# A small clear on GpSimd behind each gather of the last layer

## What is computed

```python
s = node_feats @ msg_w[:, :D].T
d = node_feats @ msg_w[:, D:].T
messages = gelu(s[:, None, :] + d[None, :, :] + msg_b)       # for each pair (i, j)
aggregated = einsum('ijd,ij->id', messages, adj)              # adj is mostly zero
new_feats = concatenate([node_feats, aggregated]) @ upd_w.T + upd_b
h = gelu(new_feats) + node_feats
x = layernorm(x + (layernorm(h) * ln_w + ln_b))
```

## Time and profile before

| | |
|---|---|
| median of three timed runs | 707.23 us |
| span of the profiled execution | 785.9 us |
| GpSimd busy in the profiled span | 333.8 us |
| VectorE busy in the profiled span | 480.0 us |

### The profile page before, as it was taken

How to read it: one execution, slowest core, us unless ns; L and a number is a source line. 1 busy time by engine, 2 the same in 40 slices (tenths; PEclk the granted TensorE clock), 3 DMA queues, 4 the chain that set the end, 5 groups by cost and what they waited for, 6 DMA issues and landing times.

```text
span 785.9 us, 6700 instructions
## 1 busy us (share of the span) xinstructions
PE 445.2 (57%) x1987; PEld 269.0 (34%) x1987; DVE 480.0 (61%) x1457; ACT 301.0 (38%) x363; POOL 333.8 (42%) x492
## 2 busy tenths in 40 slices
PE   4221118999999999999843855304504404405231
PEld 4121113444455655444632734203303303303120
DVE  2419608988946569523454559539849749748564
ACT  3565364458823316995611302203213213213131
POOL 7204502555522126400055356726636736736700
PEclk9555555999999999999865886656757757757655
DMA  8999992999712124990022211211112112111200
GB/s 317 367 424 420 398 324 110 365 398 387 298 71 72 56 72 156 425 374 1 28 73 56 73 44 43 54 30 51 47 37 50 52 32 51 50 33 50 54 8 13
DMA packets 32697, 117.20 MB, mean 149 GB/s; under 512 B 8518, under 2 KB 19636, under 8 KB 23892
## 3 DMA queue, kind: packets, MB, share of 16 engines
q1 hardware_dynamic: 19970, 78.21, 25.3%
q0 software_dynamic: 9952, 38.49, 15.5%
q10 hardware_dynamic: 2734, 0.01, 0.2%
HBM read 111.15 MB, written 5.55 MB: 148 GB/s over the span
## 4 chain that ended last, share of the span: by engine, by line
PE 40%; DVE 25%; DMA 11%; issue 10%; another core or an unknown queue 8%; ACT 3%; SPq 1%; ACTq 0%; DVEq 0%
PE ps L122 38%; DMA ring<-in_adjT_dram 11%; DVE agg L1858 4%; DVE G L1855 3%; DVE G L1843 2%; DVE A L1747 1%; DVE st L1761 1%; DVE M L1725 1%; SPq L842 1%; DVE Mh L1724 1%; DVE t L1779 1%; DVE t L1782 1%; DVE t L1781 1%; DVE yo L1788 1%
## 5 line engine op out<-in xcount | busy, mean ns | idle before, releaser
L939 POOL DMA_INDIRECT G<-near,IX x147 | 140.3, 954 | 44.8 <-issue 44.8
L122 PE MATMUL ps<-ident,agg 128*128 128x128 f32 (+1 forms) x44 | 14.3, 420 | 192.6 <-DVE agg L1858 160.2
L122 PE MATMUL ps<-ring,hwu 128*128 128x512 f32 (+3 forms) x264 | 114.3, 586 | 1.0 <-ACT hwu L1032 1.0
L122 PE MATMUL ps<-ring,xT_s 128*128 128x512 f32 (+1 forms) x264 | 108.0, 553 | 0.0
L1522 DVE FIND_INDEX8 I<-V,rows 128x8 uint32<-128x452 f32 (+1 forms) x132 | 82.1, 627 | 0.0
L939 POOL DMA_INDIRECT Go<-near,IO x44 | 43.6, 990 | 89.7 <-DVE IO L1741 59.5
L1532 DVE MAX8 V<-rows 128x8 f32<-128x452 f32 (+1 forms) x132 | 79.9, 618 | 0.8
L122 PEld LDWEIGHTS ps<-ident,agg 128*128 128x128 f32 (+1 forms) x44 | 9.4, 260 | 198.2 <-DVE agg L1858 162.6
L122 PEld LDWEIGHTS ps<-ring,hwu 128*128 128x128 f32 (+1 forms) x264 | 51.0, 203 | 63.9 <-issue 62.7
L1019 ACT ACTIVATE binT<-ring 128x2708 bf16<-128x2708 f32 (+1 forms) x22 | 53.9, 2459 | 45.2 <-DMA ring<-in_adjT_dram 45.2
L1039 ACT ACTIVATE binT<-ring 128x2708 bf16<-128x2708 f32 (+1 forms) x22 | 53.9, 2456 | 29.5 <-PE ps L122 29.5
(11 more groups left out here) (258 smaller groups left out, 843.9 us busy)
## 6 DMA issues: line engine op xcount, KB each, us to landing
ring<-in_adjT_dram SPq DMA_DIRECT2D x46, 1354.0 KB, 15.5
rows<-in_adj_dram POOLq DMA_DIRECT2D x17, 1354.0 KB, 9.5
rows<-in_adj_dram SPq DMA_DIRECT2D x4, 1354.0 KB, 23.7
G<-near,IX POOLq DMA_INDIRECT x147
xT_s<-in_xT_dram SPq DMA_DIRECT2D x1, 1354.0 KB, 6.3
near<-hwu SPq DMA_DIRECT2D x1, 1344.0 KB
out_dram<-yo SPq DMA_DIRECT2D x21, 64.0 KB
near2f<-hwu SPq DMA_DIRECT2D x5, 256.0 KB
```

Source lines behind the costliest of these rows:

```text
L122: return pe.matmul(dst, lhsT, rhs, start=start, stop=stop, skip_group_check=True)
L939: pool.indirect_dma_start(out=dst, out_offset=None, in_=table, in_offset=bass.IndirectOffsetOnAxis(ap=index, axis=0), engine_sem=o_g).then ...
```

## The change

A buffer `spare` of 128 partitions x 2 x 128 float32 is added. Behind each of the 191 gathers of layer 3 GpSimd clears one half of it (64 KB in all partitions together), the halves in turn. Each clear counts up `o_look`, and from the third on it waits first for the clear two before it (which used the same half). Nothing reads `spare`. The 22 gathers of layer 2 are as before.

```diff
+        spare = sb("spare", [P, 2, P])
...
+            pauses = itertools.count()
+
+            def pause():
+
+                k = next(pauses)
+                if k >= 2:
+                    pool.wait_ge(o_look, 9 * NB + k - 1)
+                pool.memset(spare[:, k % 2, :], 0.0).then_inc(o_look, 1)
+
             pool.wait_ge(s_n3, 16 * len(GROUPS2))
             for g in range(NG3):
...
                 for k in range(CAP):
                     gather(Go[:, g % 2, k, :], near3[:, :], IO[:, g, k:k + 1], s_go[g % 2])
+                    pause()
...
                     for k in range(TOP):
                         gather(G3[0:rn(n), n % QUEUE3, k, :], near3[:, :], IX[0:rn(n), n, k:k + 1], s_g[n % QUEUE3])
+                        pause()
```

More of the change, by code:

```diff
@@ L1 @@
+import itertools
 from contextlib import ExitStack
```

## The result

Six runs of the changed kernel have a median of 727.82 us (724.76 to 729.75), beside 707.44 us (706.32 to 710.78) for six runs of the kernel before. The ratio on record is 1.0262, 95% interval 1.023 to 1.0294, which is 18.5 us of 707.44; the two medians are 20.4 us apart. The forecast was slower, by 38 us, to 745.

A forecast was written before the change was run, and what follows sets the result against it. GpSimd's gathers (line 695.8 us) and VectorE's pairs (691) were taken to bound the kernel nearly together, GpSimd later. 191 clears x 0.20 = 38.2 us on 707.2 gave 745; likeliest range 730 to 768, 8 in 10 from 706 to 785.

The forecast's parts named there:

- The line drawn for GpSimd: GpSimd's layer 3 gathers from 434.8, 191 at 1.25 us, then 1.8 landing and 20.4 to the end: 695.8 us.
- The 11.4 us: Timed median above GpSimd's line of 695.8 us, taken as time lying around the span.
- the 78.7 us: First profile's span of 785.9 us over the timed median 707.2, taken as stalls where gathers are issued, nearly absent when timed.
- the late signals: Unnamed waits where gathers are issued, 95 us in the first profile, put down to the recording and the density of gathers.
- rival (c): Faster: late signals are real in timed runs too and the clear thins them out; 655 us, chance 0.12.
- I take 0.20 us on top of 1.25: Layer 3 gathers on GpSimd: each clear adds 0.20 us to the 1.25 between gather starts, pitch 1.45.
- rival (a): Clear hidden in the 0.30 us between gathers, or VectorE's 21.3 us pairs hold the pace: 707, up to 3 more; chance 0.18.
- (b): Clear costs twice, needing another 0.30 us gap beside an indirect DMA: 0.50 x 191 = 95.5, 803 us; chance 0.12.
- Hold-ups: Clears and VectorE's instructions delaying each other: at most 3.6 us a pair, covered by VectorE's 4.8 us to spare.
- 191 x: All 191 layer 3 clears counted at full cost on GpSimd's line: 191 x 0.20 = 38.2 us.
- the new wait: VectorE waits for a gather's landing ahead of L1843, some 4.8 us in each pair of blocks.
- The length of a pair: Two blocks of layer 3, 18 gathers: 18 x 1.45 = 26.1 us, against VectorE's 21.3.

The follow-up runs named there:

- six-gather kernel: Kernel before with the seventh gather left out for each block from block 6 on, without clears: 697.39 us, ratio 0.9854 to the kernel before.
- the second profile: The kernel before, nothing edited, profiled a second time: span 708.7 us, execution 710.41 us.

## Why the prediction was right and wrong

**Who bounds the kernel: right.** GpSimd's gathers set the pace, VectorE nearly does. The six-gather kernel shows it: 10 us go with the gathers, and VectorE's 21.25 us takes over. The line drawn for GpSimd was too short, though. It ended at 695.8; the second profile has 439.2 for the first gather (not 434.8), 172 pitches of 1.28 with the hold-ups (not 191 of 1.25) and 49.5 us behind them, 708.7 in all. The 11.4 us that I took to lie around the span are 1.7 (708.7 and 710.41).

**Where the 78.7 us lie: the use was right, the reason wrong.** I took the late signals as absent from the timed kernel, and they are. I put them down to the recording of unbroken gathers, and expected them again, if weaker, in the changed profile. Two more profiles of kernels with the gathers of before (708.7 and 705.8 us, the latter with the range tests exchanged) have none. They were of one execution. What delayed the signals there stays open; no other profile has them (whether the unprofiled execution of 2313.47 us had, can't be said), and rival (c), which lived on them, had nothing to stand on. The Trainium skill, Runtime: NRT & Kernel Launch, section The launch sequence, puts a profile's total 6.2 us above the reported time in every kernel. I had set this case's 78.7 us against it, and that was no fair test, since they were of one execution. The spans here, from first to last instruction, lie 1.8 and 1.7 us below the times (727.0 and 728.79; 708.7 and 710.41), so by this measure the sign is not that of the page either.

**"I take 0.20 us on top of 1.25, which reads the 0.30 as work of the gather": wrong, and the step that failed.** The 0.30 us are a shortest gap, and a clear uses 0.14 of it. The time from one gather's end to the next one's start is the larger of 0.30 us and clears + 0.16. For undisturbed gathers of 0.95 us that makes the pitch the larger of 1.25 and 0.95 + clears + 0.16. Six kernels stand on it:

| clear behind a gather | clear, us | pitch by the sum | pitch in the trace |
|---|---|---|---|
| none | | | 1.25 |
| 1 element | 0.12 | 1.23 | 1.25 |
| 32 | 0.14 | 1.25 | 1.25 to 1.26 |
| 128 | 0.22 | 1.33 | 1.34 |
| 128, twice | 0.37 | 1.48 | 1.48 |
| 384 | 0.43 | 1.54 | 1.55 |

The held-up clears of 1 and 32 elements are the exception: they last up to 0.43 us and the gap stays at 0.30 to 0.31. So 0.14 of the 0.30 us was room, and the clear costs 0.09 us on its own. Neither the forecast (0.20) nor rival (a) (0) nor (b) (0.50) had that; the truth was between the first two. The Trainium skill, Perfetto Trace Analysis, section DMA Instruction — SWDGE (GPSIMD), says that such a DMA has no start marker in a profile, from which I drew that the gap need not be free. The traces show 0.14 us of it free, and 0.16 us behind the clears of 128 elements; whether these 0.16 are work of the gather, no run shows.

**Hold-ups: priced too low.** I called them at most 3.6 us a pair and covered, but priced them for VectorE. They fall mostly on GpSimd, which has no cover. The clears take 3.7 us more than 191 x 0.22, most of it beside VectorE's range tests, and the gathers are 188.6 us busy in place of 185.8, 6.5 us in all.

**"191 x": wrong by the tail.** The chain leaves GpSimd at gather 173, the last of block 18, in both kernels, as its starts at 659.16 and 677.17 show. The last 18 are covered by VectorE. The sum that should have stood: 172 pitches x 0.09 = 15.5 us, and some 4 us of hold-ups up to there, 19.5 us, which is what the two chains differ by. The forecast was 191 x 0.20 = 38.2: the price of a clear is 18.9 too much over the 172 (0.11 each), the tail 3.8, and the hold-ups are missing. Right were the sign and the place of the new wait (L1843 of before, 3.5 us a pair against 4.8). The length of a pair is right to within 1.0 us (25.1 against 26.1) by luck: 18 x 1.34 is 24.1, and some 1.0 us of hold-ups, which the forecast left out, makes up half of the error.

## What to carry to other kernels

Where an engine issues one instruction after another with the same idle time between them, that time can be in part free and in part taken, as here (0.14 and 0.16 us of 0.30); measure what fits by putting in something of two or three sizes. When a profile's span is far from the timed runs, profile once more before any row of it is explained. And follow the chain to the instruction where it leaves the paced engine: only what lies ahead of it multiplies.

## What was not expected of the hardware

- A gather of 128 rows of 512 B starts 0.30 us after the end of the one before it when nothing lies between them, also behind a gather that was held up to 1.31 us, and still does with a clear of 0.12 us in between, whose wait and signal are free as well.
- A clear by GpSimd of 0.22 us lasts 0.40 to 0.50 us in ten of the 15 cases in which it overlaps a VectorE range test with a scalar, and 0.22 to 0.23 in all 18 once that test takes two tensors.
- A clear of 1 or 32 elements that is held up to 0.31 to 0.43 us doesn't delay the next gather, which starts 0.30 to 0.31 us after the last one's end; one of 128 elements does.
- In one execution of the kernel before, signals came up to 27 us late (TensorE idle from 528.71 - 31.22 = 497.5, its result taken up by L1747 at 524.23), and in no other profile of this study. One execution of the kernel with two clears took 2313.47 us in place of 751 and was not profiled.
